# A block's row maxima transposed four tiles past its last chunk instead of two, in a macaron transformer block

## The chip, the cores and the metric

The kernel runs on one core of a Trainium2 chip. The metric is the device time of one execution in microseconds; the time before is 3196.67 us, the median of three runs (3193.45 to 3202.14).

## The reference

A half-weighted feed-forward layer, attention, and the same feed-forward layer again, each with a residual and a layer norm, on 2048 tokens of width 512. The feed-forward layers dequantize four-bit weights (4096 wide) and apply a gelu gate. Attention, on which the change acts, is this:

```python
scores = jnp.einsum('bhqd,bhkd->bhqk', q, k) / math.sqrt(Hd)       # 16 heads of 32
causal = jnp.triu(jnp.full((S, S), -jnp.inf, dtype=scores.dtype), k=1)
attn = jax.nn.softmax(scores + causal[None, None], axis=-1)
out = jnp.einsum('bhqk,bhkd->bhqd', attn, v)
```

## The kernel before

The program has three parts: the first feed-forward layer, `attend` (projections, attention, output projection), and the second feed-forward layer. The change touches `attend` alone.

In attention the 2048 queries of a head are cut into four blocks of 512, and the keys into 16 tiles of 128. A head consists of 40 tiles (TILES), each the scores of one key tile against the queries of one block; block b has 4(b + 1) of them, and the causal ones on the diagonal are narrower (512, 384, 256, 128 columns). For each tile t TensorE computes transposed scores (L1211, and a mask at L1215 where the tile is on the diagonal), ScalarE takes the exponential (L1283), and TensorE multiplies with the values. The 24 tiles off the diagonal are split in two parts: ScalarE writes the exponential a second time, rounded (L1285), GpSimd subtracts the two (L1324, probs_low), and TensorE runs two fast products (L1231, L1234). The 16 tiles on the diagonal are kept whole and use fp32 products (L1228). TensorE computes scores four tiles ahead of the values (AHEAD = 4); the scores have three banks.

The exponentials need each row's maximum before the scores are computed: minus the maximum, in two parts, sits in rows 96 and 97 of `queries`, against ones in `keys`, so that the matmul at L1211 subtracts it. These maxima are found one head in advance. While the tiles of one head run, the scores of the next head are computed in the other orientation, in 40 chunks of up to 512 keys for 128 queries (`max_chunk`, L699, and a mask at L703). VectorE reduces each chunk to its maxima (`take_max`, L721). When the last chunk of a block has been reduced, VectorE does three small steps (`split_max`): it reduces the chunks' maxima (L729), copies them rounded (L734) and subtracts (L736). TensorE then transposes the result with four small matmuls (`rows`, L712), and ScalarE copies the two rows into `queries` (`store_rows`, L742). `rows` waits for the subtraction.

The order is written out by formula. `chunks_of_slot(t)` says which chunks TensorE issues at tile t, MAXED_AT at which tile the last chunk of a block lies, and ROWS_AT at which tile the transposes follow. Within a tile TensorE issues the scores of tile t + 4, the chunks, the transposes if there are any, and the values product of tile t. ScalarE has the exponentials of tile t + 4, the row copy, and at the first tile behind a block the copy of its outputs (L1292). VectorE has the chunks and then `split_max`. ITEMS lists chunks and transposes in this order, and they take three banks of PSUM in turn (`max_bank_of`): before an item is issued, `wait_for_max_bank` waits until the item three places before it has been reduced or copied out. All queues are in order.

The first head's maxima are computed inside `project_in`, where ITEMS is spread over the projection tiles by `head_items_after`. The fifteen others lie in attention; the loop turns every three heads, and the sixteenth head has no successor and so no chunks. SyncE loads heads and stores outputs, and its order depends on none of these constants.

Of the kernel before, what the change touches and what calls it, by code (L numbers as in the profile page):

```python
# [579 lines left out]
SLOTS = len(TILES)  # L580
# [7 lines left out]
SPLIT = [t for t in range(SLOTS) if t not in WHOLE]  # L588


def chunks_of_slot(t):

    return [m for m in range(SLOTS) if m * (SLOTS - 2) // SLOTS == t]


MAXED_AT = {[t for t in range(SLOTS) if b * (b + 1) * 2 + 4 * (b + 1) - 1 in chunks_of_slot(t)][0]: b
            for b in range(NTB)}
ROWS_AT = {t + 2: b for t, b in MAXED_AT.items()}

ITEMS = [item for t in range(SLOTS)  # L600
         for item in [("chunk", m) for m in chunks_of_slot(t)] + ([("rows", ROWS_AT[t])] if t in ROWS_AT else [])]
MAX_BANKS = 3

# [523 lines left out]
def attention(nc, bank, o_parts, sums, inverses, w_out, b_out, heads, o):  # L1127
    with ExitStack() as ctx:
# [67 lines left out]
        def _(pe):  # L1196
# [22 lines left out]
            def with_values(hp, s, t):  # L1219
                b, kt = TILES[t]  # L1220
                i = s % 3
                if t in FIRST_OF_BLOCK:
                    pe.wait_ge(out_free, 12 * hp + (4 * s + b + 1))
                pe.wait_ge(probs_ready, 120 * hp + (SLOTS * s + t + 1))
                off = max(0, kt * P - b * TB)
                out = out_bank[b % 2][0:VCOLS, off:TB]
                if t in WHOLE:
                    last = pe.matmul(out, f32(values[i][:, kt, :]), probs[:, t % RING, 0:TB - off],  # L1228
                                     start=(t in FIRST_OF_BLOCK), stop=(t in LAST_OF_BLOCK), skip_group_check=True)
                else:  # L1230
                    pe.matmul(out, values[i][:, kt, :], probs_high[:, t % RING, 0:TB - off],  # L1231
                              start=(t in FIRST_OF_BLOCK), stop=False, skip_group_check=True)
                    pe.wait_ge(probs_low_ready, 3 * len(SPLIT) * hp + (len(SPLIT) * s + SPLIT.index(t) + 1))
                    last = pe.matmul(out, values[i][:, kt, :], probs_low[:, t % RING, 0:TB - off],  # L1234
                                     start=False, stop=(t in LAST_OF_BLOCK), skip_group_check=True)
                if t in LAST_OF_BLOCK:
                    last.then_inc(out_ready, 1)

            def head(hp, s, has_next):
                for t in range(SLOTS):  # L1240
                    if t + AHEAD < SLOTS:
                        scores(hp, s, t + AHEAD)
                    elif has_next:
                        scores(hp, s + 1, t + AHEAD - SLOTS)
                    if has_next:
                        for m in chunks_of_slot(t):
                            heads.max_chunk(pe, hp, s + 1, m)
                        if t in ROWS_AT:
                            heads.rows(pe, hp, s + 1, ROWS_AT[t])
                    with_values(hp, s, t)  # L1250
# [26 lines left out]
        def _(act):  # L1277
            def exps(hp, s, t):
                b, kt = TILES[t]
                width = TB - max(0, kt * P - b * TB)  # L1280
                act.wait_ge(scores_ready, 120 * hp + (SLOTS * s + t + 1))
                source = score_bank[(SLOTS * s + t) % SCORE_BANKS][:, 0:width]
                last = act.activation(probs[:, t % RING, 0:width], source, ACT.Exp, scale=SM_SCALE)  # L1283
                if t in SPLIT:
                    last = act.activation(probs_high[:, t % RING, 0:width], source, ACT.Exp, scale=SM_SCALE)  # L1285
                last.then_inc(probs_ready, 1)
# [8 lines left out]
            def head(hp, s, has_next):  # L1295
                for t in range(SLOTS):
                    if t + AHEAD < SLOTS:
                        exps(hp, s, t + AHEAD)
                    elif has_next:
                        exps(hp, s + 1, t + AHEAD - SLOTS)  # L1300
                    if has_next and t in ROWS_AT:
                        heads.store_rows(act, hp, s + 1, ROWS_AT[t])
                    if t - 1 in LAST_OF_BLOCK:
# [262 lines left out]
```

## Time and profile before

| | |
|---|---|
| median of three runs | 3196.67 us |
| the profiled execution | 3196.54 us |
| its span | 3194.7 us |
| TensorE busy | 3015.3 us (94%) |
| VectorE busy | 1945.8 us (61%) |
| ScalarE busy | 1263.3 us (40%) |
| GpSimd busy | 1264.9 us (40%) |

The span runs from the first to the last instruction. Attention takes the stretch from about 1297 to 2010 us. Matmuls are pipelined and are drawn with their whole latency, so a busy TensorE isn't one at its peak: a matmul of 512 columns is drawn as 0.39 us, and the next one starts 0.23 us after it. PE is TensorE, PEld its weight load, DVE VectorE, ACT ScalarE, POOL GpSimd.

### The profile page before, as it was taken

The numbers are of one execution on the slowest core, as the hardware profiler recorded it, in microseconds if no ns is written. First come the engines' busy times: TensorE is split into PE (matmuls) and PEld (weight loads), VectorE is DVE, ScalarE is ACT, GpSimd is POOL, SyncE is SP. The second block draws the span as 40 slices with busy tenths as digits, with TensorE's granted clock in tenths as the row PEclk, the third lists the DMA queues.
The fourth block names the chain that finished last, engine by engine and source line by source line (L and its number), as shares of the span: only waits on it lengthen the run. The fifth ranks groups of instructions, "written<-read, shape, count | busy, mean of one in ns | idle before, by whom it ended". The sixth has DMA issues, their size and how long they took to land. (4 is left out here: it accounts for less than half of the span.)

```text
span 3194.7 us, 40306 instructions
## 1 busy us (share of the span) xinstructions
PE 3015.3 (94%) x13408; PEld 2316.5 (73%) x13408; DVE 1945.8 (61%) x2795; ACT 1263.3 (40%) x2213; POOL 1264.9 (40%) x880
## 2 busy tenths in 40 slices
PE   5999999999999989999999999669999999999999
PEld 3788888888888758555555555447888888888887
DVE  7666656665666465666666664476666566665664
ACT  4322222222222242677777778233222222222222
POOL 4322222222222175566666767433222222222221
PEclk9999999999999989999999999789999999999999
DMA  2000000000000039322222240310000000000001
GB/s 92 21 27 27 26 20 26 26 26 20 20 26 14 28 93 253 105 47 66 65 64 49 54 105 23 114 40 20 27 27 26 20 23 23 26 26 20 26 13 53
DMA packets 123898, 144.37 MB, mean 45 GB/s; under 512 B 71904, under 2 KB 72160, under 8 KB 120480
## 3 DMA queue, kind: packets, MB, share of 16 engines
q1 hardware_dynamic: 123256, 142.70, 15.8%
q8 instruction: 42, 0.69, 0.1%
q10 hardware_dynamic: 552, 0.59, 0.1%
q14 instruction: 48, 0.39, 0.0%
HBM read 105.26 MB, written 38.01 MB: 45 GB/s over the span
## 5 line engine op out<-in xcount | busy, mean ns | idle before, releaser
L60 PE MATMUL psum<-ffn_x_high,ffn_w_high 128*128 128x512 f32 x2048 | 803.3, 392 | 17.2 <-DVE ffn_gelu L388 17.2
L525 POOL TENSOR_TENSOR ffn_inner<-ffn_gelu,ffn_inner 128x512 fp32r<-128x512 f32 x256 | 346.2, 1352 | 1156.4 <-ACT ffn_inner L470 1156.4
L61 PE MATMUL psum<-ffn_x_low,ffn_w_high 128*128 128x512 f32 x2048 | 798.9, 390 | 0.0
L62 PE MATMUL psum<-ffn_x_high,ffn_w_low 128*128 128x512 f32 x2048 | 798.6, 390 | 0.0
L1324 POOL TENSOR_TENSOR probs_low<-probs,probs_high 128x512 fp32r<-128x512 f32 x384 | 483.5, 1282 | 223.7 <-ACT probs_high L1285 223.2
L378 DVE SCALAR_TENSOR_TENSOR ffn_gelu<-ffn_gelu,psum 128x512 f32<-128x512 f32 x256 | 176.0, 688 | 599.1 <-ACT ffn_gelu L463 599.0
L721 DVE TENSOR_REDUCE chunk_max<-psum 128x1 f32<-128x512 f32 (+3 forms) x640 | 383.4, 610 | 217.2 <-PE psum L699 113.0
L60 PEld LDWEIGHTS psum<-ffn_x_high,ffn_w_high 128*128 128x128 f32 x2048 | 386.2, 189 | 103.0 <-DVE ffn_gelu L388 20.9
L61 PEld LDWEIGHTS psum<-ffn_x_low,ffn_w_high 128*128 128x128 f32 x2048 | 386.0, 188 | 81.6 <-issue 2.0
L62 PEld LDWEIGHTS psum<-ffn_x_high,ffn_w_low 128*128 128x128 f32 x2048 | 385.7, 188 | 80.5
L60 PE MATMUL psum<-ffn_inner,ffn_w_high 128*128 128x512 f32 x1024 | 398.6, 389 | 0.2
L61 PE MATMUL psum<-ffn_inner,ffn_w_high 128*128 128x512 f32 x1024 | 398.4, 389 | 0.0
L62 PE MATMUL psum<-ffn_inner,ffn_w_low 128*128 128x512 f32 x1024 | 398.4, 389 | 0.0
L1283 ACT ACTIVATE probs<-psum 128x512 f32<-128x512 f32 (+3 forms) x640 | 341.4, 548 | 96.6 <-PE psum L1211 57.3
L463 ACT ACTIVATE ffn_gelu<-psum 128x512 f32<-128x512 f32 x256 | 152.8, 597 | 530.9 <-PE psum L62 530.9
L519 POOL TENSOR_TENSOR ffn_w_low<-ffn_weight,ffn_w_high 128x1024 fp32r<-128x1024 f32 x96 | 232.1, 2418 | 329.5 <-ACT ffn_w_high L456 329.5
L394 DVE SCALAR_TENSOR_TENSOR x<-psum,x 128x512 f32<-128x512 f32 x512 | 321.3, 683 | 16.0 <-PE psum L62 16.0
L470 ACT ACTIVATE ffn_inner<-ffn_gelu 128x512 fp32r<-128x512 f32 x256 | 161.9, 632 | 381.2 <-DVE ffn_gelu L388 381.2
L1211 PE MATMUL psum<-queries,keys 98*128 98x512 f32 (+3 forms) x640 | 298.5, 467 | 3.0 <-ACT probs_high L1285 2.1
L382 DVE SCALAR_TENSOR_TENSOR ffn_gelu<-ffn_gelu,psum 128x512 f32<-128x512 f32 x256 | 176.2, 688 | 180.0 <-ACT ffn_gelu L465 180.0
L456 ACT ACTIVATE ffn_w_high<-ffn_weight 128x1024 fp32r<-128x1024 f32 x96 | 102.0, 1062 | 398.9 <-DVE ffn_weight L369 398.9
L699 PE MATMUL psum<-keys,queries 96*128 96x512 f32 (+3 forms) x640 | 248.9, 398 | 1.0 <-DVE chunk_max L721 0.7
(124 smaller groups left out, 3989.3 us busy)
## 6 DMA issues: line engine op xcount, KB each, us to landing
ffn_words<-packed SPq DMA_DIRECT2D x96, 256.0 KB
ffn_word_scales<-scales SPq DMA_DIRECT2D x96, 256.0 KB
qk_parts<-parts SPq DMA_DIRECT2D x32, 512.0 KB, 4.4
queries<-qk_parts SPq DMA_DIRECT2D x48, 256.0 KB, 4.6
keys<-qk_parts SPq DMA_DIRECT2D x48, 256.0 KB, 6.6
v_parts<-parts SPq DMA_DIRECT2D x16, 512.0 KB, 6.1
values<-v_parts SPq DMA_DIRECT2D x16, 512.0 KB, 10.9
o_parts<-heads_out SPq DMA_DIRECT2D x64, 128.0 KB
```

The source lines that it names most:

```text
L60: pe.matmul(out, w_high, x_high, start=first, stop=False, skip_group_check=True)
L61: pe.matmul(out, w_high, x_low, start=False, stop=False, skip_group_check=True)
L62: return pe.matmul(out, w_low, x_high, start=False, stop=last, skip_group_check=True)
L382: dve.scalar_tensor_tensor(out=cubic[m], in0=square[m], scalar=1.0, in1=gate_bank[m], op0=ALU.add, op1=ALU.mult)\
L394: dve.scalar_tensor_tensor(out=x[:, k, cols(tb, TB)], in0=down_bank[k], scalar=FFN_BACK, in1=x[:, k, cols(tb, TB)], op0=ALU.mult, op1=ALU. ...
L519: pool.tensor_tensor(w_low[s][:, :, piece, :], weight[:, q % 2, :, :], f32(w_high[s][:, :, piece, :]), ALU.subtract).then_inc(w_low_ready, 1)
L525: pool.tensor_tensor(inner[:, tb % 2, m, 1, :], product[m], f32(inner[:, tb % 2, m, 0, :]), ALU.subtract)\
L699: last = pe.matmul(out[:, 0:width], self.queries[i][0:self.STACK, cols(qt, P)], self.keys[i][0:self.STACK, c * TB:c * TB + width], start=T ...
L721: dve.tensor_reduce(self.chunk_max[:, b % 2, qt % 4, c:c + 1], self.max_bank[max_bank_of(s, ("chunk", m))][:, 0:width], AX.X, ALU.max).the ...
L1211: last = pe.matmul(out[:, 0:width], keys[i][0:ROWS, cols(kt, P)], queries[i][0:ROWS, q0:q0 + width], start=True, stop=(kt < 4 * b), skip_g ...
L1283: last = act.activation(probs[:, t % RING, 0:width], source, ACT.Exp, scale=SM_SCALE)
L1324: pool.tensor_tensor(probs_low[:, t % RING, 0:width], probs[:, t % RING, 0:width], f32(probs_high[:, t % RING, 0:width]), ALU.subtract)\
```

## The change

The distance between the last chunk of a block and its transposes becomes a constant, ROWS_AFTER, and goes from two tiles to four. The chunks of a head are spread over the first SLOTS - ROWS_AFTER = 36 tiles, not 38. SLOTS is 40.

```diff
+ROWS_AFTER = 4
+
+
 def chunks_of_slot(t):
 
-    return [m for m in range(SLOTS) if m * (SLOTS - 2) // SLOTS == t]
+    return [m for m in range(SLOTS) if m * (SLOTS - ROWS_AFTER) // SLOTS == t]
 
 
 MAXED_AT = {[t for t in range(SLOTS) if b * (b + 1) * 2 + 4 * (b + 1) - 1 in chunks_of_slot(t)][0]: b
             for b in range(NTB)}
-ROWS_AT = {t + 2: b for t, b in MAXED_AT.items()}
+ROWS_AT = {t + ROWS_AFTER: b for t, b in MAXED_AT.items()}
```

## Rows read from the trace of the kernel before

**Rows 1.** Waits in attention, 1300 to 2010 us: total us, times, longest.

```profile
PEld psum L712 <- issue: 57.9, 50, 2.2
PE psum L712 <- DVE max_parts L736: 48.6, 45, 1.9
PEld psum L1234 <- POOL probs_low L1324: 10.0, 17, 1.0
PEld psum L699 <- DVE chunk_max L721: 3.1, 13, 0.2
```

**Rows 2.** Timeline of TensorE over one head: start us, us, what, idle before.

```profile
1481.14 0.40 PE L712 MATMUL psum<-ident_r,max_parts 128*2 128x128 f32 x4 [0.28 <-DVE max_parts L736]
...
1486.78 0.23 PE L703 MATMUL psum<-query_mask_b,ident_b 128*128 128x128 bf16 x1
1488.01 0.40 PE L712 MATMUL psum<-ident_r,max_parts 128*2 128x128 f32 x4 [1.00 <-DVE max_parts L736]
...
1496.26 0.40 PE L712 MATMUL psum<-ident_r,max_parts 128*2 128x128 f32 x4
...
1504.96 0.39 PE L699 MATMUL psum<-keys,queries 96*128 96x512 f32 x1
...
1505.73 0.39 PE L1211 MATMUL psum<-queries,keys 98*128 98x512 f32 x1
...
1506.66 0.22 PE L1211 MATMUL psum<-queries,keys 98*128 98x128 f32 x1
...
1506.77 0.48 PE L699 MATMUL psum<-keys,queries 96*128 96x512 f32 x1
1509.09 0.40 PE L712 MATMUL psum<-ident_r,max_parts 128*2 128x128 f32 x4 [1.85 <-DVE max_parts L736]
1509.33 1.02 PE L1228 MATMUL psum<-probs,values 128*65 128x512 f32 x2
...
1510.42 0.39 PE L699 MATMUL psum<-keys,queries 96*128 96x512 f32 x1
```

**Rows 3.** VectorE: all of L734 and L736 (ns min/median/max), then one head's timeline.

```profile
L734 DVE CAST max_parts<-minus_max x64: 170/503/1282, 1244.3 to 1970.5; 128x4 fp32r<-128x4 f32 x64
L736 DVE TENSOR_TENSOR max_parts<-minus_max,max_parts x64: 162/164/1205, 1245.0 to 1970.7; 128x4 fp32r<-128x4 f32 x64
...
1486.54 1.14 DVE L734 CAST max_parts<-minus_max 128x4 fp32r<-128x4 f32 x1
...
1487.81 0.89 DVE L721 TENSOR_REDUCE chunk_max<-psum 128x1 f32<-128x512 f32 x2
...
1495.19 0.36 DVE L734 CAST max_parts<-minus_max 128x4 fp32r<-128x4 f32 x1
...
1506.48 1.27 DVE L734 CAST max_parts<-minus_max 128x4 fp32r<-128x4 f32 x1
1507.79 1.18 DVE L736 TENSOR_TENSOR max_parts<-minus_max,max_parts 128x4 fp32r<-128x4 f32 x1
1508.89 1.28 DVE L721 TENSOR_REDUCE chunk_max<-psum 128x1 f32<-128x512 f32 x2
```

**Rows 4.** Timeline of GpSimd beside block 2's steps.

```profile
1505.20 3.74 POOL L1324 TENSOR_TENSOR probs_low<-probs,probs_high 128x512 fp32r<-128x512 f32 x3 [0.34 <-ACT probs_high L1285]
```

**Rows 5.** Groups by line, 1346 to 1972 us: count, busy us, mean ns, idle.

```profile
L1324 POOL TENSOR_TENSOR probs_low<-probs,probs_high 128x512 fp32r<-128x512 f32 x336 | 423.3, 1282 | 201.5 <-ACT probs_high L1285 200.9
```

**Rows 6.** Windows of 1 us: us, busy PE PEld DVE ACT POOL, clock, DMA.

```profile
1375.00:1376.00 1.00, 1.00 (x3) 0.34 (x1) 0.31 (x1) 0.27 (x1) 0.00 (x0) 0.50 0.00 0
1846.00:1847.00 1.00, 1.00 (x5) 0.52 (x3) 0.25 (x2) 0.78 (x2) 0.66 (x1) 0.50 1.15 260
```

**Rows 7.** Timeline of TensorE: block 3's transposes of three heads in a row.

```profile
1346.30 0.40 PE L712 MATMUL psum<-ident_r,max_parts 128*2 128x128 f32 x4 [0.28 <-DVE max_parts L736]
...
1391.58 0.40 PE L712 MATMUL psum<-ident_r,max_parts 128*2 128x128 f32 x4 [0.30 <-DVE max_parts L736]
...
1435.16 0.40 PE L712 MATMUL psum<-ident_r,max_parts 128*2 128x128 f32 x4 [0.27 <-DVE max_parts L736]
```

## The prediction

> **What bounds the kernel now.** I read the list of waits first, for the stretch that holds the fifteen heads whose maxima are prepared inside attention. In it TensorE's largest wait on another engine is the one in front of the transposes at L712: 45 times, 48.6 us, on VectorE's last step of a block's maxima (L736). Its weight loader stood 57.9 us before the same line [rows 1]; a matmul is drawn longer than the time until the next can start, so the wait list counts a stall some 0.1 to 0.25 us short. Every other wait of TensorE there is small: 3.1 us for chunk maxima and 10.0 us for GpSimd's probs_low, and the latter falls mostly in the last head, which has no chunks and is outside this change [rows 1].
>
> The timeline of TensorE over one head then shows where the waits are [rows 2]. I measure each gap from the start before it plus the pace of that instruction (about 0.06 us for a 128-column mask, 0.23 us for 512 columns). Block 0 (tile 4): 1486.84 to 1488.01, 1.17 us. Block 1 (tile 12): none, its row has no bracket. Block 2 (tile 23): 1507.00 to 1509.09, 2.09 us. Block 3 (tile 39): the bracket at 1481.14 has 0.28 us, plus the 0.17 by which a mask drawn as 0.23 overstates its pace, 0.45 us. A head loses 3.71 us; fifteen lose 55.7 us, which agrees with the 57.9 us.
>
> Why the maxima are late is in VectorE's rows [rows 3]. The copy at L734 and the subtraction at L736 each handle four numbers per partition. The copy took 1.14 us in block 0 and 0.36 in block 1; in block 2 the copy took 1.27 and the subtraction 1.18 us, while GpSimd ran three products back to back from 1505.20 to 1508.94 [rows 4]. So VectorE is done 4.01 us after TensorE issues the block's last chunk (1504.96 to 1508.97), and only after that come the chunks that queue behind it on VectorE: chunk 24 is taken by 1509.58, chunk 25 by 1510.17.
>
> **The change, part by part.** No instruction is added or taken away: 40 chunks, four groups of transposes and four row copies per head stay, and no transfer moves. Costs can only come from order. By the formula the last chunks of the blocks are issued at tiles 2, 9, 20, 35 (before 2, 10, 21, 37), and the transposes at 6, 13, 24, 39 (before 4, 12, 23, 39). So every block has four tiles of cover, before two. Tiles with two chunks are 0, 9, 18, 27 (before 0, 19), and tiles 36 to 38 have none.
>
> The rows are not the only thing that waits, though. Three banks hold chunks and rows in turn, so TensorE's next chunk needs the chunk three items before it taken. That is the next limit, and I work it out for each block.
>
> Block 2. Before, TensorE's work from the last chunk to the transposes is 1504.96 to 1507.00, 2.04 us. After, the same chunk sits in tile 20, and up to chunk 27 in tile 24 there is in addition one split tile (1505.73 to 1506.66, 0.93), tile 23's values product with tile 24's scores (1509.33 to 1510.42, 1.09), and 0.17 because tile 20's product is a 384-column fp32 one (three quarters of some 0.85) where tile 21's took 0.47 [rows 2]. That is 4.23 us. The transposed maxima are ready at 4.01 in both, if the copy and the subtraction collide with GpSimd again as in [rows 3]. But chunk 27 needs chunk 24 taken (1509.58 - 1504.96 = 4.62), and the transposes need chunk 25 taken (5.21 by the same row). TensorE waits about 0.4, then, after some 0.15 of chunk, 0.45 to 0.5: in all 0.97. Saved: 2.09 - 0.97 = 1.12.
>
> Block 0. Tile 4's values take 0.47 (half of a 0.93 tile that has four equal matmuls), tile 5 (384 columns of scores with a mask, a chunk, 128 columns of fp32 values) some 0.69, tile 6 up to the transposes 0.42. TensorE is there at 1486.84 + 1.58 = 1488.42. The transposes now come three items behind chunk 5, taken by 1488.70 (start 1487.81 plus 0.89 for two) [rows 3]. It waits some 0.33 with the semaphore's step. Saved: 0.84.
>
> Block 1. Nothing is waited for now. The two chunks of tile 9 put VectorE some 0.5 us further back, and TensorE's four tiles cover that. I take 0; the upper end stands under the rivals. Block 3. Tile 35 to 39 cover the 0.45 us wholly, with three tiles without a chunk between. Saved: 0.45.
>
> Behind the waits on other engines: ScalarE's copy of the rows (L742) stands in order between exponentials, so it waits for the transposes as TensorE does; it gets shorter waits too. GpSimd's products need 1282 ns each, 24 to a head, 30.8 us [rows 5], against 43.5 us of head. Its lead is refilled by the stalls: where these shrink, it still has the same tiles ahead, since it starves when TensorE stands. I cost both at 0; the cover is the 43.5 - 30.8 us, and what it costs if it fails is the third rival. The first head's maxima run under the projections; there the last transposes follow the last chunk directly in both versions, so that stall is unchanged.
>
> Sum: (1.12 + 0.84 + 0.45) = 2.41 us x 15 = 36.2 us.
>
> **The clock.** A second term rests on the granted clock. In [rows 6] it is 0.50 (1.2 GHz of the two levels) in the stretch behind a block 2 wait, and again behind block 0's wait of the head that follows a loop's turn. I count seven such stretches, three behind a block 2 wait and four at the turn of the loop over three heads, all right behind a wait for L712. The cost of one comes from the starts of block 3's transposes [rows 7]: 1346.30 to 1391.58 is 45.28 us with one in it, 1391.58 to 1435.16 is 43.58 without, so some 1.75 us. That most vanish with the idle time ahead of them is my reading; the bounds are none and all seven (12.2 us). With waits shortened but not gone in block 2, I take five: 8.8 us.
>
> Total 45 us. The profiled execution took 3196.54 us (span 3194.7), 0.1 us under the median of 3196.67, so the two need no correction: 3196.5 - 45 = **3151.5 us**.
>
> **The rivals.**
> Forecast, half of the stalls and most clock stretches gone: 3151.5 us, its own range 3138 to 3165. Chance 0.62.
>
> All gone: if VectorE meets GpSimd at a better moment, the banks never stop TensorE. The shortest copy and subtraction took 0.17 and 0.16 us [rows 3], so what block 2 has is not their own length. Then 3.71 x 15 = 55.7, plus 12.2 of clock: 3128.6 us. Against it stands that GpSimd is three products deep at that point [rows 4]. Chance 0.18.
>
> Block 1 turns bad: its last two chunks now come together and are followed at once by the copy and the subtraction; if both meet GpSimd as in block 2, VectorE is 2.45 us on them where it was 0.52 (0.36 and the median 0.16 of L736), and TensorE would wait about 0.75 at chunk 15 and 0.45 at the transposes, 1.2 per head. With no clock gained, 3196.5 - (2.41 - 1.2) x 15 = 3178 us. For it speaks that GpSimd is the busiest neighbour; against, that it has gaps between products around block 1 (the copy there took 0.36, 0.19 over the shortest). Chance 0.10. Beside this stands a rule of the Trainium skill, SBUF — State Buffer, section "Who interferes with whom": GpSimd and VectorE share a port pair as an exclusive lock, taken by a copy or by an operation with two SBUF inputs, and whoever starts first holds it for the whole instruction. The durations in [rows 3] agree. By that rule moving the transposes removes none of VectorE's lateness, and the phase in which it meets GpSimd decides block 1; at its worst that is this rival's 3178 us, and at its best the time of the rival before.
>
> Hidden anyway: GpSimd or ScalarE sets the pace once TensorE doesn't stand. GpSimd's 30.8 us against 41.1 us of the new head speaks against it. Then 3196 us. Chance 0.05.
>
> Slower: the bank takes the place of the rows everywhere. If VectorE is over 2 us late with the first chunk behind its split in each of the first three blocks, TensorE stands at the chunk instead: blocks 0 and 2 lose what they lost, block 1 loses 1.2 us in addition, block 3 gains its 0.45: +0.75 x 15 = 11 us, 3208 us. It decides where the bank's chunk, three items back, lies behind the copy on VectorE, which it does; but the four tiles have been computed above to cover most of it. Chance 0.05.
>
> **How the numbers follow.** A measurement of this kernel can tell about 0.3% (9.6 us) from no change. Faster by more: the first three, 0.90; within: 0.05; slower: 0.05. The range reaches from near the full gain to the bad block 1, 3128 to 3179.
>
> **What would show it.** In the profile after: the wait of L712 on L736 gone or under 5 us; new waits of L699 or L712 on L721, about 0.4 to 1 us in block 2 and 0.3 in block 0, some 15 to 20 us in all; starts of block 3's transposes 41.1 us apart, before 43.5; stretches at clock 0.50 at most two; VectorE's copy in block 2 still over 1 us. A wait before L712 that still names L736 with over 20 us, or a block 1 with over 0.5 us of gap, would make the prediction wrong on the step named; a head of 43 us with new waits on L1324 would mean that GpSimd took over.

## The result, and the profile after

The changed kernel takes 3144.13 us (median of four runs, 3144.0 to 3147.62) against 3198.28 us for the kernel before in the runs beside it: ratio 0.9838, 95% interval 0.9826 to 0.9851. Forecast were 3151.5 us, range 3128 to 3179. The profiled executions were 3196.54 us before and 3144.05 us after, with spans of 3194.7 and 3142.2 us: 52.5 us less.

The list of waits of the kernel after, in attention from 1300 to 1960 us (total us, times, longest), beside [rows 1]. Lines have moved by three: L715 is L712 before, L702 is L699, L724 is L721, L739 is L736.

```profile
PEld psum L702 <- DVE chunk_max L724: 18.1, 30, 0.7
...
PEld psum L1237 <- POOL probs_low L1327: 10.4, 19, 1.0
...
PEld psum L715 <- DVE chunk_max L724: 5.0, 15, 0.3
PE psum L715 <- DVE chunk_max L724: 2.9, 15, 0.2
...
PEld psum L715 <- issue: 0.9, 6, 0.2
```

The wait of the transposes on the maxima (48.6 us before) is no longer in the list. In its place TensorE waits 45 times for a chunk to be taken, so for a bank: three times a head, at two chunks (the 30 of L702) and at block 2's transposes (the 15 of L715). The weight loader's two rows add up to 23.1 us. GpSimd's part is the same 10 us, in the last head.

The timeline of TensorE over one head (start us, us, what, idle before), answering to [rows 2]:

```profile
1465.50 0.43 PE L715 MATMUL psum<-ident_r,max_parts 128*2 128x128 f32 x4
...
1470.77 0.48 PE L1214 MATMUL psum<-queries,keys 98*128 98x512 f32 x1
1471.09 0.22 PE L702 MATMUL psum<-keys,queries 96*128 96x128 f32 x1
...
1472.37 0.48 PE L1214 MATMUL psum<-queries,keys 98*128 98x512 f32 x1
1472.98 0.39 PE L702 MATMUL psum<-keys,queries 96*128 96x256 f32 x1
1473.20 0.23 PE L706 MATMUL psum<-query_mask_b,ident_b 128*128 128x128 bf16 x1
1473.24 0.43 PE L715 MATMUL psum<-ident_r,max_parts 128*2 128x128 f32 x4
...
1480.91 0.41 PE L715 MATMUL psum<-ident_r,max_parts 128*2 128x128 f32 x4
...
1487.65 0.40 PE L702 MATMUL psum<-keys,queries 96*128 96x512 f32 x1
...
1490.91 1.02 PE L1231 MATMUL psum<-probs,values 128*65 128x512 f32 x2
1491.37 0.80 PE L1214 MATMUL psum<-queries,keys 98*128 98x512 f32 x1
1492.22 0.33 PE L702 MATMUL psum<-keys,queries 96*128 96x128 f32 x1
1492.38 0.23 PE L706 MATMUL psum<-query_mask_b,ident_b 128*128 128x128 bf16 x1
1492.82 0.40 PE L715 MATMUL psum<-ident_r,max_parts 128*2 128x128 f32 x4 [0.20 <-DVE chunk_max L724]
...
1506.43 0.43 PE L715 MATMUL psum<-ident_r,max_parts 128*2 128x128 f32 x4
```

By the same reckoning as in the prediction, block 0 has 0.39 us left, not at its transposes but just ahead of them: 0.29 at chunk 7, which starts 0.61 us behind the scores where the chunk one tile earlier starts 0.32 behind them (1470.77 to 1471.09), and 0.10 at chunk 7's mask (1472.98 plus 0.12 for 256 columns, to 1473.20). Block 1 has none. Block 2 has 0.22 us at chunk 27 (1492.00 to 1492.22), 0.10 at its mask (1492.28 to 1492.38) and 0.38 at the transposes (1492.44 to 1492.82), 0.70 in all. Block 3 has none. In the four heads behind the turn of the loop block 0 has 0.3 us more. Block 3's transposes are 40.93 us apart, before 43.6. The two ends of the chain, from the timeline of VectorE in block 2, answer to [rows 3]:

```profile
1489.18 1.15 DVE L737 CAST max_parts<-minus_max 128x4 fp32r<-128x4 f32 x1
1490.36 1.20 DVE L739 TENSOR_TENSOR max_parts<-minus_max,max_parts 128x4 fp32r<-128x4 f32 x1
1491.49 0.68 DVE L724 TENSOR_REDUCE chunk_max<-psum 128x1 f32<-128x512 f32 x1
```

VectorE is as late as before: 1487.65 to 1491.56 is 3.91 us, before 4.01. The lateness was covered, not removed. No stretch at clock 0.50 is left between block 3's first transposes at 1342 us and the last at 1918 us, where there were seven. The windows between these transposes, of the kernel after and of the kernel before, have it as the third number from the end, 1.00 and 0.98:

```profile
1342.00:1918.00 576.00, 568.25 (x2916) 351.27 (x2915) 416.36 (x729) 491.18 (x1009) 423.53 (x336) 1.00 0.29 66
1346.00:1971.40 625.40, 578.48 (x2918) 359.90 (x2918) 412.46 (x730) 488.36 (x1009) 423.29 (x336) 0.98 0.26 61
```

### The profile page after: what moved, and what is told of

Read it like the earlier page. It is cut to its first block and busy times, and to the rows that moved or that the text cites. A ratio compares the mean times of both kernels' runs of the same rounds, so it can differ in the third digit from the quotient of the medians.

```text
span 3142.2 us, 40306 instructions
## 1 busy us (share of the span) xinstructions
PE 3002.4 (96%) x13408; PEld 2306.5 (73%) x13408; DVE 1947.2 (62%) x2795; ACT 1266.8 (40%) x2213; POOL 1264.4 (40%) x880
## 5 line engine op out<-in xcount | busy, mean ns | idle before, releaser
L62 PE MATMUL psum<-ffn_x_high,ffn_w_low 128*128 128x512 f32 x2048 | 798.9, 390 | 0.0
L724 DVE TENSOR_REDUCE chunk_max<-psum 128x1 f32<-128x512 f32 (+3 forms) x640 | 370.2, 606 | 161.3 <-PE psum L706 81.2
L62 PEld LDWEIGHTS psum<-ffn_x_high,ffn_w_low 128*128 128x128 f32 x2048 | 385.9, 188 | 80.6
L62 PE MATMUL psum<-ffn_inner,ffn_w_low 128*128 128x512 f32 x1024 | 398.4, 389 | 0.0
L702 PE MATMUL psum<-keys,queries 96*128 96x512 f32 (+3 forms) x640 | 242.3, 396 | 5.1 <-DVE chunk_max L724 2.4
```

The source lines that it names most:

```text
L62: return pe.matmul(out, w_low, x_high, start=False, stop=last, skip_group_check=True)
L702: last = pe.matmul(out[:, 0:width], self.queries[i][0:self.STACK, cols(qt, P)], self.keys[i][0:self.STACK, c * TB:c * TB + width], start=T ...
L724: dve.tensor_reduce(self.chunk_max[:, b % 2, qt % 4, c:c + 1], self.max_bank[max_bank_of(s, ("chunk", m))][:, 0:width], AX.X, ALU.max).the ...
```

## The experiments

**Distance alone and spreading alone.** The change has two edits in one constant. In the first run the transposes come four tiles behind, and the chunks stay spread over 38 (block 3's have only two tiles left, 37 to 39); in the second the chunks are spread over 36, and the distance stays two.

```diff
 e1_far_only, against the kernel before
+ROWS_AFTER = 4
...
-ROWS_AT = {t + 2: b for t, b in MAXED_AT.items()}
+ROWS_AT = {min(t + ROWS_AFTER, SLOTS - 1): b for t, b in MAXED_AT.items()}
 e2_spread_only, against the kernel before
+ROWS_AFTER = 4
...
-    return [m for m in range(SLOTS) if m * (SLOTS - 2) // SLOTS == t]
+    return [m for m in range(SLOTS) if m * (SLOTS - ROWS_AFTER) // SLOTS == t]
```

> The transposes come four tiles behind a block's last chunk (block 3's stay at tile 39), but the chunks are spread over 38 tiles as before. My theory (the distance does it, block by block): blocks 0 and 2 gain as in the change, block 3's 0.45 us a head stays, 15 x 0.45 = 7 us over the change's 3144 us: about 3151 us, no stretch at clock 0.50 inside the fifteen heads. Rival (the spreading over 36 tiles does it): about 3196 us.

> The chunks are spread over 36 tiles, but the transposes stay two tiles behind a block's last chunk. My theory: the waits at L712 stay (1.2 us in block 0, 2.1 in block 2, 0.45 in block 3), and block 1, whose last two chunks now share a tile, gets one of about 0.5 to 1 us: 3198 to 3212 us, with several stretches at clock 0.50. Rival (spreading does it): about 3150 us.

Distance alone: 3160.08 us, ratio 0.9888 (0.9872 to 0.9905). Spreading alone: 3199.04 us, ratio 1.0009 (0.9999 to 1.0019), so no change that can be told. The distance does it, but it was worth 9 us less than I expected. About half of that is at the banks: without the spreading TensorE has less work between a block's last chunk and chunk 27 (1494.26 to 1498.42, 4.16 us, where the change has 4.35). The timeline of TensorE in e1_far_only, block 2:

```profile
1494.26 0.39 PE L702 MATMUL psum<-keys,queries 96*128 96x512 f32 x1
...
1498.96 0.33 PE L702 MATMUL psum<-keys,queries 96*128 96x128 f32 x1 [0.39 <-DVE chunk_max L724]
...
1499.55 0.40 PE L715 MATMUL psum<-ident_r,max_parts 128*2 128x128 f32 x4 [0.20 <-DVE chunk_max L724]
...
1513.11 0.40 PE L715 MATMUL psum<-ident_r,max_parts 128*2 128x128 f32 x4 [0.30 <-DVE max_parts L739]
```

The gap at chunk 27 is 0.54 us where the change has 0.22, the gaps at its mask and at the transposes and that of block 0 are the same, and block 3 keeps its 0.45. Block 2's 0.32 us a head are 5 of the 9 us. Another 2 us lie ahead of the first chunk, where the kernels are the same (it starts at 1238.2 us, in the change at 1236.3), so they are a difference between two executions; the rest I did not place. So spreading is worth nothing that can be told while the transposes wait for the maxima, and 16 us once they don't, 7 of them because it makes room for block 3's distance. In the second run the expected stall in block 1 is there (the first row, of its timeline; the second is block 2):

```profile
1495.96 0.22 PE L715 MATMUL psum<-ident_r,max_parts 128*2 128x128 f32 x1 [0.57 <-DVE max_parts L739]
...
1508.92 0.41 PE L715 MATMUL psum<-ident_r,max_parts 128*2 128x128 f32 x4 [1.52 <-DVE max_parts L739]
```

Its waits on L739 add up to 58.5 us, 10 us more than before, and yet the time is the same. It has one stretch at clock 0.50 where the kernel before has seven; six fewer are some 10 us. Why it has so few I can't say: its waits in block 0 at the turn of the loop are as long (1.34 us) as those behind which the clock fell each time before.

**Three and six tiles.** The constant alone.

> Distance three, chunks over 37 tiles; block 2 has two chunks in the tile of its transposes. My theory: block 0 keeps about 0.5 us, block 2 about 1.7 (first at the bank of chunk 27, then at that of the transposes), block 3 none: 1.6 us saved a head, 24 us, and some of the clock stretches (5 us): about 3165 us. If only the lateness of the maxima counted (4.01 us behind the last chunk) and no bank, block 2 would keep 0.7 us and the time would be near 3150 us.

> Distance six, chunks over 34 tiles. My theory: once L712 waits for nothing but a bank, VectorE's lateness reaches TensorE through the banks wherever the transposes stand, so nothing more is gained: block 2 keeps 0.6 to 1 us at a chunk: 3142 to 3155 us. Rival (the distance to the maxima still decides): the remaining 0.6 us of block 2 and what block 0 has go, about 3130 us.

Three: 3166.31 us, ratio 0.9907 (0.9891 to 0.9924), near the reckoning with banks (3165) and not near that with the lateness of the maxima alone (3150). That it is so near is in part luck: a head became 1.36 us shorter (42.29 us for 43.65), not 1.6, and all seven clock stretches went (11 to 12 us), where I had taken 5 us for them. Its waits:

```profile
PEld psum L702 <- DVE chunk_max L724: 22.4, 15, 1.5
...
PEld psum L715 <- DVE chunk_max L724: 19.5, 30, 1.2
...
PE psum L702 <- DVE chunk_max L724: 15.9, 15, 1.1
PE psum L715 <- DVE chunk_max L724: 12.8, 30, 0.9
```

No wait of the fifteen heads names the maxima. Six: 3152.13 us, ratio 0.9863 (0.9847 to 0.988). The time was as expected, my place for it was wrong. Block 2 has no gap left; the stall is in block 0, where two chunks now share tile 5: some 0.85 us at chunk 7 and its mask, and 0.3 us more in the four heads behind the turn of the loop, of which this is one:

```profile
1437.48 0.39 PE L702 MATMUL psum<-keys,queries 96*128 96x256 f32 x1 [0.89 <-DVE chunk_max L724]
```

Beside it TensorE's weight loader waits for GpSimd in 33 places, 17.8 us, where the change has 19 and 10.4 us. Yet a head takes 41.05 us, only 0.1 more than in the change, so the fifteen heads lose 2 of the 8 us. Some 5 us are lost earlier, where the first head's maxima run under the projections: from the first chunk to the first values product it takes 69.6 us, in the change 64.4, with one wait of 2.87 us for ScalarE's copy of the rows (L745), again for a bank. From its list of waits, 1230 to 1350 us:

```profile
PE psum L702 <- ACT queries L745: 2.9, 1, 2.9
```

More distance is not better in itself; where the pairs of chunks fall, and which bank the transposes hold, decide what it gives.

**Why VectorE is late.** The copy is replaced by a second reduction of the chunk maxima, which writes the same rounded values; once in the changed kernel, once in the kernel before.

```diff
-        dve.tensor_copy(self.max_parts[:, b % 2, :, 0], self.minus_max[:, b % 2, :]).then_inc(self.max_steps, 1)
+        dve.tensor_reduce(self.max_parts[:, b % 2, :, 0], self.chunk_max[:, b % 2, :, 0:b + 1], AX.X, ALU.max,
+                          negate=True).then_inc(self.max_steps, 1)
```

> The change, with VectorE's copy (the rounded high part of the maxima) replaced by a second reduction of the chunk maxima that writes the same values. The theory that VectorE's copy and subtraction stand behind GpSimd's products, and a reduction does not: in block 2 the first step is no longer held (0.17 us for 1.15), the subtraction is held by the product then running, VectorE is some 1.2 us earlier and the 0.7 us gap at the banks of block 2 goes; in block 0 and 1 the subtraction inherits the copy's wait (about 0.8 to 1 us on it), nothing gained there. 15 x 0.7 = 10 us under the change: about 3134 us. Rival (the copy is slow in itself, because it follows two small steps): the reduction takes as long, 3144 us.

> The kernel before (two tiles), with the same replacement of the copy by a reduction. By the same theory: block 0 keeps 1.1 us, because the subtraction waits for the same product; block 2 falls from 2.1 to about 0.9 us; 15 x 1.2 = 18 us, and the three clock stretches behind block 2 with it (5 us): about 3173 us. Rival (the copy is slow in itself): 3196 us.

After: 3135.14 us, ratio 0.9814 (0.9798 to 0.9831). Before: 3160.13 us, ratio 0.9892 (0.9875 to 0.9908). The instructions on the tile of the maxima (ns: shortest, median, longest), the copy of the changed kernel first, then e5_after_reduced:

```profile
L737 DVE CAST max_parts<-minus_max x64: 169/922/1352, 1242.6 to 1916.3; 128x4 fp32r<-128x4 f32 x64
...
L737 DVE TENSOR_REDUCE max_parts<-chunk_max x64: 158/164/171, 1243.3 to 1906.0; 128x4 fp32r<-128x4 f32 x16, 128x4 fp32r<-128x8 f32 x16, 128x4 fp32r<-128x12 f32 x16, 128x4 fp32r<-128x16 f32 x16
L740 DVE TENSOR_TENSOR max_parts<-minus_max,max_parts x64: 162/955/1286, 1243.5 to 1906.2; 128x4 fp32r<-128x4 f32 x64
```

The reduction is never held, 171 ns at most, where the copy took up to 1352 (1282 in [rows 3]); the subtraction behind it inherits the wait, median 955 ns for 165. This is the behaviour that the Trainium skill states in SBUF — State Buffer, "Who interferes with whom": a copy can contend with GpSimd, an operation with two SBUF inputs contends with a GpSimd instruction that reads SBUF, a reduction never does on this chip. In e5_after_reduced block 2's gap is gone whole (0.70 us) and block 0's by 0.25 of 0.39, for which I had expected nothing; but a head is only 0.64 us shorter. The weight loader now waits for GpSimd's products 45 times in the fifteen heads, 11.0 us in all, where in the change it did so twice (0.3 us): the next wait begins to show, though it is not shown that it takes back the missing 0.3 us a head.

In the kernel before, the time fell 13 us further than expected. L712 waits 22.7 us for the maxima instead of 48.6, and all seven clock stretches are gone, where I had expected three to go. I had 1.1 and 0.9 us for blocks 0 and 2; by the timeline block 2 has 0.85 and block 0 0.98, but only 0.3 in the four heads behind the turn of the loop, where it had 1.5. 26 us and 12 us are 38, measured are 36.

**GpSimd's products made short.** The other way to the same question: the kernel before, with the products cut to 64 of up to 512 columns. The rest of the low parts is zero and so left out of the result.

```diff
-                width = TB - max(0, kt * P - b * TB)
+                width = TB // 8
...
+            pool.memset(f32(probs_low[:]), 0.0).then_inc(heads.filled, 1)
+            pool.wait_ge(heads.filled, 7)
```

> The kernel before, with GpSimd's products in attention cut to 64 of up to 512 columns (the low parts of the other columns are left at zero: they are left out of the result). If VectorE's lateness comes from GpSimd's products, its copy and subtraction take 0.17 us each everywhere, blocks 0 and 2 lose their stalls (1.17 and 2.07, at most 0.15 left), block 3 keeps its 0.45, and no clock stretch is left: 3.1 x 15 + 12 = 58 us, and the last head, which waits for GpSimd, some 5 us besides: about 3133 us. If the copy is slow in itself: above 3185 us.

3141.95 us, ratio 0.9835 (0.9818 to 0.9851). The copy, with nothing else changed on VectorE:

```profile
L734 DVE CAST max_parts<-minus_max x64: 169/171/769, 1245.8 to 1915.7; 128x4 fp32r<-128x4 f32 x64
```

Its median falls from 503 to 171 ns, and L712 waits 4.3 us for the maxima, 15 times: block 3's. So GpSimd's products are the cause of the lateness, shown from both sides. The 9 us that are missing are in two places: block 3's transposes are 40.70 us apart, not 40.3, and attention's last values product starts 4.9 us earlier than in the changed kernel (1949.1 for 1954.0) while the second feed-forward layer's first L62 does so by 1.6 only (2071.6 for 2073.2). What the output projection waits for there I did not follow.

**One tile.** The other way on the same scale, mainly for the clock.

```diff
-ROWS_AT = {t + 2: b for t, b in MAXED_AT.items()}
+ROWS_AT = {t + 1: b for t, b in MAXED_AT.items()}
```

> The kernel before with the transposes one tile behind a block's last chunk (tiles 3, 11, 22, 38), so every stall grows by the work of the tile that no longer covers it: block 0 from 1.2 to about 1.8 us, block 1 from none to about 0.85, block 2 from 2.1 to about 2.85, block 3 from 0.45 to about 1.1; 2.8 us a head more, 43 us: 3239 us with as many clock stretches as before. My theory of the clock (a stretch at 0.50 follows a long enough stall at the transposes, and costs 1.75 us) adds more of them behind block 2: between 10 and 20 in the fifteen heads instead of seven, so 3244 to 3262 us. Rival (they belong to the turn of the loop and chance, not to the stall): four to seven of them, 3234 to 3242 us.

3261.92 us, ratio 1.0209 (1.0192 to 1.0227). Timeline of TensorE, blocks 0 and 2 of one head:

```profile
1506.20 0.40 PE L712 MATMUL psum<-ident_r,max_parts 128*2 128x128 f32 x4 [1.58 <-DVE max_parts L736]
...
1528.80 0.40 PE L712 MATMUL psum<-ident_r,max_parts 128*2 128x128 f32 x4 [2.72 <-DVE max_parts L736]
```

There are 19 stretches at clock 0.50: one behind each of the fifteen waits of block 2, and one in each of the four heads that follow the loop's turn, behind block 0's (1.93 us). Block 1 now stands too, 0.95 us at its own transposes on L736 (expected 0.85). A head has some 3 us more of stall; with 44 us of it and twelve more stretches (20 us) the time would be 3258 us from the 3193.7 us of the kernel before beside it.

**What is left.** Chunks placed by hand, with a tile without one where the bank behind the split is needed, alone and with the reduction. HOLES are the tiles with no chunk, DOUBLES those with two, and CHUNKS_AT is the list that a loop makes of them.

```diff
+HOLES, DOUBLES = (6, 24), (0, 8, 12, 15, 25, 28)
...
-    return [m for m in range(SLOTS) if m * (SLOTS - ROWS_AFTER) // SLOTS == t]
+    return CHUNKS_AT[t]
...
-ROWS_AT = {t + ROWS_AFTER: b for t, b in MAXED_AT.items()}
+ROWS_AT = {7: 0, 14: 1, 25: 2, 39: 3}
```

> The change, with the chunks placed by hand: a tile without a chunk four tiles behind the last chunk of block 0 (tile 6) and of block 2 (tile 24), two chunks in tiles 8, 12, 15, 25 and 28, transposes at 7, 14, 25 and 39. If what is left of the stall sits at the banks (a chunk that needs the first chunk behind the split taken), both gaps go, 0.25 in block 0 and 0.7 in block 2: about 3131 us. Rival (the remaining time is a bound of ScalarE or GpSimd, so closing gaps moves the wait elsewhere): 3140 to 3150 us.

> Holes and reduction together. If both act on the same wait, the two gains don't add: within 3 us of the better of the two alone, 3128 to 3134 us. If they act on separate waits they add up to some 3122 us.

Alone: 3138.22 us, ratio 0.9822 (0.9805 to 0.9838), half of the gain expected. The interval touches that of the change (0.9826 to 0.9851), but the traces show the gain as well: block 3's transposes are 40.42 us apart for 40.93. The wait at the chunks is gone, but my own order put chunks 27 and 28 ahead of block 2's transposes, which then need chunk 26 taken:

```profile
PEld psum L724 <- DVE chunk_max L733: 6.2, 15, 0.4
```

(L724 is the transposes, L733 the chunk maxima in this kernel.) Together: 3133.48 us, ratio 0.9808 (0.9791 to 0.9824). The gains don't add, as they would not on one wait. It is the lowest median of all, and beats both kernels; from the reduction alone (0.9814) it can't be told apart.

## Why the prediction was right

**The waits.** The wait at L712 went to nothing and a smaller one on the banks came in its place, as forecast; only block 0's stands one item earlier than I had it, at chunk 7 and its mask and not at the transposes. By block, saved against forecast: block 0 0.78 us (0.84), block 1 none (none), block 2 1.39 (1.12), block 3 0.45 (0.45). The sum by the timeline is 2.62, by the distance of the heads 2.65; forecast were 2.41. Fifteen heads give 40 us for the 36.2. The term that was mis-sized is block 2's rest, 0.97 forecast and 0.70 measured. In part that is the prediction's own sum: its two waits, about 0.4 and 0.45 to 0.5, add up to 0.85 to 0.90, not to 0.97. The rest of it is small errors that all close the gap: chunk 24 is taken 4.52 us behind the last chunk (forecast 4.62), TensorE arrives after 4.35 (4.23), and what remains is a difference of two such numbers.

**The clock.** Forecast five stretches fewer, 8.8 us; all seven went. That I held two back for block 2's rest was the second mis-sized term, and the price of one was a little high: 45.28 and 43.58 us are 1.70 apart, not 1.75, and the second of these heads has another place in the loop. Heads of the same place take 45.28 and 45.26 with a stretch and 43.65 without, so 1.6 us, and seven are 11 to 12 us. I took the count from one profiled execution of each kernel. In the 13 runs beside e1_far_only the kernel before spreads from 3191.4 to 3200.5 us, while the ten of e2_spread_only, with one stretch in its profile, lie within 2.6 us; that the number of stretches changes from run to run would explain it, but is not shown.

**Where the time went.** From the first to the last values product of attention it was 704.6 us and is 653.2, 51.3 us less, which is the 40 and the 11 to 12. Of the 52.5 us of the spans 1.9 lie ahead of the first chunk (1238.17 us before, 1236.30 after), where nothing was changed: that is a difference between two executions. Both terms of the forecast were low, so nothing cancelled; the measured time fell within the range of the forecast because that had 13 us on either side of 3151.5.

**The rivals.** "All gone" was wrong in that the banks do stop TensorE (e3_three shows a kernel in which nothing else does). "Block 1 turns bad" was open until the trace: the copy there does take 0.90 us now, for 0.36 before, but the subtraction behind it is free, and the four tiles cover it; with two tiles between, in e2_spread_only, it shows as a stall. "Hidden anyway" has nothing for it at four tiles; at six, and with the reduction, the waits on GpSimd begin to grow. "Slower" needed the bank to take over whole; it took over 1.09 of 3.71 us.

**What I did not see.** That spreading and distance depend on each other: the same two edits are worth 36 us and nothing that can be told alone, and 54 together.

## What to carry to other kernels

When a wait on a side chain stalls the main engine, ask two things of moving the consumer away: what the producer of the side chain is itself held by (here another engine's long operations), and which ring of buffers runs through the same producer, because that ring stalls next and caps the gain. Then check where work lands in pairs; the spacing of the items counted as much as the distance. A stall on TensorE may cost more than its length: count the stretches at the lower clock that follow it.

## What the runs showed of the hardware

The clock fell from 2.4 to 1.2 GHz (granted clock 0.50) in or behind waits of TensorE of 1.3 to 2.7 us. Counted in the fifteen heads, by the kernel's longest waits as drawn:

| run | waits at the transposes | stretches at 0.50 in or behind them |
|---|---|---|
| e9_one | 2.72 us, block 2, 15 times | 15 |
| | 1.93 us, block 0 at the loop's turn, 4 times | 4 |
| | 1.6 us, block 0 elsewhere, 10 times | 0 |
| the kernel before | 1.85 us, block 2, 15 times | 3 |
| | 1.35 us, block 0 at the loop's turn, 4 times | 4 |
| e2_spread_only | 1.52 us, block 2, 15 times | 0 |
| | 1.34 us, block 0 at the loop's turn, 4 times | 1 |
| the change and the eight other kernels | none over 1.1 us | 0 |

The longest waits had it always and those up to 1.1 us never; in between the length alone does not tell it, and what else does no run shows. Of each kernel there is one profiled execution. A stretch costs about 1.6 us, nearly as much as the wait ahead of it.

The other surprise was the size of the hold: an operation on four numbers per partition takes 0.17 us alone and up to 1.35 beside GpSimd's products of 1.28 us. Taking the first of two such operations out of a chain left the second to wait: in the changed kernel the subtraction's median rose from 0.16 to 0.96 us. Only in block 2, where both had been held one after the other, did this shorten the chain by a whole hold.
